# A recommendation tower on one core: top layers in four sets, and one PSUM factor filled by DMA and ScalarE in place of a matmul

## The chip, the cores and the metric

The kernel runs on one core of a Trainium2 chip. The metric is the device time of one execution in microseconds (us). The profile of an execution also has a span, from the first to the last instruction, which is a little shorter than the device time.

## The reference, cut to what matters

512 samples each look up 32 rows of 16 numbers (one row from each of 32 tables). Three layers of products follow, and each layer's output is summed over the 16 columns; the 3 x 64 sums with 16 dense inputs go through three top layers. All is float32.

```python
e = stack([tbl_0[ids[:, 0]], ..., tbl_31[ids[:, 31]]], axis=1)      # 512 x 32 x 16
xk = x0 = e
for W in (W0, W1, W2):                     # 32 x (32 or 64) x 64
    xk = relu(einsum('bmd,bhd,mhk->bkd', x0, xk, W))
    outs.append(sum(xk, axis=2))           # 512 x 64 each
h = concatenate([concatenate(outs, axis=1), dense_ctx], axis=1)     # 512 x 208
h = maximum(h @ W_top1 + b_top1, 0.0)      # 512 x 512
h = maximum(h @ W_top2 + b_top2, 0.0)      # 512 x 256
y = h @ W_top3                             # 512 x 1
```

## The kernel before, in words

The 512 samples are two halves, t = 0 and 1, that are worked side by side in the two halves of TensorE's columns (`side_by_side`, L566). Each half is cut into nine sets p = 0 to 8 of `SAMPLES` = 16, 24, 32 (six times), 24 samples (L16); a set of 32 samples has 512 columns, one of 24 has 384, one of 16 has 256.

A set passes three layers n = 0, 1, 2. Their order is `STAGES` (L41 to L48): (1, p), then (0, p + 1), then (2, p - 1), for each p. So while set p is in layer 1, its successor is in layer 0 and its predecessor in layer 2. "Stage (n, p)" below means layer n of set p.

In each stage a left factor (each of the layer's input rows repeated 4 times over the partitions) is multiplied with rotated copies of the set's gathered rows, and TensorE multiplies the products with the weights and adds them up in `result[n]`. The rotated copies come in two forms (q = 0 and 1, four chunks each): `r0_forms` and `r1_forms`. The left factor has two forms as well, j = 0 (input rows 0 to 31) and j = 1 (rows 32 to 63). VectorE makes units of up to four chunks (`products`, L503, the instruction is L519); GpSimd makes some of the chunks of form j = 1 in pairs (L314 to L328, how many is `pool_chunks`). Layers 1 and 2 have three or four VectorE units (0 and 1 are j = 0, 2 and 3 are j = 1), layer 0 has one. `z_vector` has three buffers (NV), so VectorE can be up to three units ahead of TensorE.

Where the left factor comes from:
- Form 1 lies in PSUM bank `left[:, t, 1]`. For layer 0 ScalarE copies it from `h_form` (`copy_h`, L354), which a DMA loaded with the repetition. For layers 1 and 2 ScalarE issues a DMA that repeats rows 32 to 63 of the previous layer's output in `xj1_forms` (`load_xj1`, L386), and later copies it to PSUM (`copy_xj1`, L364). GpSimd reads `xj1_forms` directly.
- Form 0 of layers 1 and 2 lies in `left[:, t, 0]`. TensorE makes it: `select` (L598) multiplies the previous layer's output with a 0/1 matrix. select(2, p - 1) stands after unit 1 of stage (1, p), select(1, p + 1) after unit 1 of stage (2, p - 1).

ScalarE's order is written out by hand (L443 to L493). For each p: copy_xj1(1, p); copy_h(p + 1); relu(1, p); copy_xj1(2, p - 1); relu(0, p + 1); load_xj1(1, p + 1); relu(2, p - 1); load_xj1(2, p). Each copy waits for its DMA and for the PSUM bank to come free, and what stands behind it waits too.

SyncE's queue (L271 to L290) stores each set's gathered rows to DRAM (`store_x0`), then loads `h_form`, the two `r0_forms` and the two `r1_forms` (1 MB each for 32 samples). The stores wait for the gathers (L309), which GpSimd issues: 20 at once for sets 0 and 1, 16 for set 2 behind a wait for the first select (L335 to L338), and then 8 behind each stage's GpSimd products (L340 to L344). The r loads also wait until layer 2 of the set three before is done.

The top layers are made in two parts, both in tiles cut from a free slot of `r0_forms` (L151 to L163). `early` (L608 on TensorE, L417 on ScalarE) takes sets 0 to 6 (400 columns) in seven steps, spread over stages (2, 7) and (2, 8). The rest, sets 7 and 8 (112 columns, `LATE`), follows when the last layer 2 is done (L668 to L690).

Of the kernel before, what the change touches and what calls it, by code (L numbers as in the profile page):

```python
# [15 lines left out]
SAMPLES = [16, 24] + [32] * 6 + [24]  # L16
NP = len(SAMPLES)
# [9 lines left out]
EARLY = NP - 2  # L27
EARLY_COLUMNS, LATE = 2 * START[EARLY], 2 * (START[NP] - START[EARLY])

# [19 lines left out]
LAYERS = [_stage for _stage in STAGES if _stage[0] > 0]  # L49

# [64 lines left out]
def build(nc, table, ids, base, w0, w0_mirror, not_twice, w12, select, dense, w_top1, b_top1, w_top2, b_top2, w_top3,  # L115
# [3 lines left out]
    with ExitStack() as ctx:  # L119
# [7 lines left out]
        table_base = sb("table_base", [128, GATHERS_BEFORE[-1]], I32)  # L127
# [8 lines left out]
        z_square = sb("z_square", [128, 2, C])  # L136
# [13 lines left out]

        spare = r0_forms[:, (NP - 3) % R0_SLOTS].rearrange("p t s c -> p (t s c)")  # L151
        spare_at = [0]

        def from_spare(columns):
            at = spare_at[0]
            spare_at[0] += columns
            return spare[:, at:at + columns]

        top_in = from_spare(2 * B).rearrange("p (f t c) -> p f t c", f=2, t=2)
        hidden1 = from_spare(N1 * EARLY_COLUMNS).rearrange("p (k c) -> p k c", k=N1)  # L160
        hidden2 = from_spare(N2 * EARLY_COLUMNS).rearrange("p (k c) -> p k c", k=N2)
        late1 = from_spare(N1 * LATE).rearrange("p (k c) -> p k c", k=N1)
        late2 = from_spare(N2 * LATE).rearrange("p (k c) -> p k c", k=N2)  # L163
        y_sb = h_form[0:1, 0].rearrange("o (t b) -> o t b", t=2)
# [4 lines left out]
        y_psum = ctx.enter_context(nc.psum_tensor("y_psum", [128, B], F32))  # L169
        early_banks = [y_psum, result[0]]  # L170
        late1_psum = [left[:, t, 0, 0:2 * LATE].rearrange("p (k c) -> p k c", c=LATE) for t in range(2)]
        late2_psum = [left[:, t, 1] for t in range(2)]
        late3_psum = result[1]
# [14 lines left out]
        selected = sem("selected")  # L188
        left_copied = sem("left_copied")
# [8 lines left out]
        early_in_ready = sem("early_in_ready")  # L198
        early_summed = sem("early_summed")
        early_ready = sem("early_ready")  # L200
# [29 lines left out]
        def _(sp):  # L230
# [61 lines left out]
            for k, samples in enumerate((slice(0, START[EARLY]), slice(START[EARLY], B // 2))):  # L292
                sp.wait_ge(y_ready, k + 1)
                sp.dma_start(out.rearrange("(t b) o -> o t b", t=2)[:, :, samples], y_sb[:, :, samples]
                             ).then_inc(y_stored, 16)
            sp.wait_ge(y_stored, 32)

        @block.gpsimd
        def _(pool):
# [31 lines left out]
            nc.gpsimd.tensor_tensor(row_index[:], ids_all[:], table_base[:], ALU.add).then_inc(index_ready, 1)  # L331
# [15 lines left out]
        def _(act):  # L347
# [24 lines left out]
            def relu(n, p):  # L372
# [4 lines left out]
                if p > 0:  # L377
                    act.wait_ge(x_summed[n], p)
                    if n < 2:

                        act.wait_ge(selected, LAYER_AT[n + 1, p - 1] + 1)
                        for t in range(2):
                            act.wait_ge(xj1_loaded[n][t], 16 * p)
                nc.scalar.activation(x_sb[n][:, 0:columns(p)], result[n][:, 0:columns(p)], ACT.Relu).then_inc(x_ready[n], 1)  # L384

# [14 lines left out]
            def top_block(n, t, pairs, ready):  # L400
                samples = slice(START[pairs[0]], START[pairs[1]])
                nc.scalar.activation(top_in[K * (n % 2):K * (n % 2) + K, n // 2, t, samples],  # L402
                                     d_sums[K * t:K * t + K, n, samples], ACT.Copy).then_inc(ready, 1)

            def y_out(pairs, bank):
                first, end = START[pairs[0]], START[pairs[1]]
                nc.scalar.activation(y_sb[:, :, first:end],
                                     bank[0:1, 0:2 * (end - first)].rearrange("o (t b) -> o t b", t=2),
                                     ACT.Copy).then_inc(y_ready, 1)

            def early_inputs():
                for n in range(3):
                    act.wait_ge(x_summed[n], EARLY)
                    for t in range(2):
                        top_block(n, t, (0, EARLY), early_in_ready)

            def early(k):  # L417
                act.wait_ge(early_summed, k + 1)
                bank = early_banks[k % 2]
                if k < N1:  # L420
                    nc.scalar.activation(hidden1[:, k], bank[:, 0:EARLY_COLUMNS], ACT.Relu,
                                         bias=b_top1_sb[:, k:k + 1]).then_inc(early_ready, 1)
                elif k < N1 + N2:
                    nc.scalar.activation(hidden2[:, k - N1], bank[:, 0:EARLY_COLUMNS], ACT.Relu,
                                         bias=b_top2_sb[:, k - N1:k - N1 + 1]).then_inc(early_ready, 1)
                else:
                    y_out((0, EARLY), bank)

            act.dma_start(table_base[:], base).then_inc(ids_loaded, 16)
# [32 lines left out]

            act.wait_ge(z_vector_ready, 2 * vector_after((2, EARLY - 1)))
            act.wait_ge(z_pool_ready, 2 * pool_after((2, EARLY - 1)))
            act.dma_start(top_in[K:K + D, 1], dense).then_inc(top_loaded, 16)
            early_inputs()
            copy_xj1(2, last - 1)
            relu(1, last)
            load_xj1(2, last)
            act.wait_ge(top_loaded, 16 * 7)  # L470
            for k in range(N1):
                early(k)
            copy_xj1(2, last)
            for n in range(2):
                act.wait_ge(x_summed[n], NP)
                for t in range(2):
                    top_block(n, t, (EARLY, NP), late_in_ready)
            relu(2, last - 1)
            for k in range(N1, N1 + N2 + 1):
                early(k)  # L480
# [3 lines left out]
            top_block(2, 0, (EARLY, NP), late_in_ready)  # L484
            act.wait_ge(late1_summed, 1)
            for k in range(N1 // 2):
                nc.scalar.activation(late1[:, k], late1_psum[0][:, k], ACT.Relu,
                                     bias=b_top1_sb[:, k:k + 1]).then_inc(late1_by_scalar, 1)
            act.wait_ge(late2_summed, 1)
            nc.scalar.activation(late2[:, 0], late2_psum[0][:, 0:LATE], ACT.Relu,  # L490
                                 bias=b_top2_sb[:, 0:1]).then_inc(late2_by_scalar, 1)
            act.wait_ge(late3_summed, 1)
            y_out((EARLY, NP), late3_psum)  # L493

        @block.vector
        def _(dve):
# [6 lines left out]
            def products(n, p, k):  # L503
# [4 lines left out]
                for t in range(2):  # L508
# [6 lines left out]
                    elif k == 0:  # L515
                        dve.wait_ge(selected, LAYER_AT[n, p] + 1)
# [37 lines left out]
            nc.vector.tensor_copy(top_in[0:K, 1, 1, START[EARLY]:START[NP]],  # L554
                                  d_sums[K:2 * K, 2, START[EARLY]:START[NP]]).then_inc(late_in_ready, 1)
            dve.wait_ge(late1_summed, 2)
            for k in range(N1 // 2, N1):
                nc.vector.tensor_scalar(late1[:, k], late1_psum[1][:, k - N1 // 2], b_top1_sb[:, k:k + 1], 0.0,
                                        ALU.add, ALU.max).then_inc(late1_by_vector, 1)
            dve.wait_ge(late2_summed, 2)  # L560
            nc.vector.tensor_scalar(late2[:, 1], late2_psum[1][:, 0:LATE], b_top2_sb[:, 1:2], 0.0,
# [3 lines left out]
        def _(pe):  # L565
# [28 lines left out]
            def squares(p):  # L594
                pe.wait_ge(z_square_ready, 2 * p + 2)
                side_by_side(0, p, w0_sb[:, 4], z_square, False, True).then_inc(z_square_used, 1)
# [11 lines left out]
            def early(k):  # L608
                if k == 0:
                    pe.wait_ge(top_loaded, 16 * 7)  # L610
                    pe.wait_ge(early_in_ready, 6)
                if k == 1:
                    pe.wait_ge(x_ready[0], NP)
                if k >= 2:
                    pe.wait_ge(early_ready, k - 1)
                bank = early_banks[k % 2]
                if k < N1:
                    for half, rows in enumerate((128, K + D)):
                        done = nc.tensor.matmul(  # L619
# [122 lines left out]
```

## Time and profile before

| what | value |
|---|---|
| device time, median of 3 runs | 353.35 us (351.65 to 353.98) |
| device time of the profiled execution | 353.74 us |
| its span | 351.9 us |
| TensorE matmul busy | 305.4 us, 87% |
| VectorE busy | 274.2 us, 78% |
| GpSimd busy | 254.2 us, 72% |
| ScalarE busy | 61.6 us, 18% |
| mean granted TensorE clock | 0.985 of full |

The device time is 1.84 us over the span: what lies around the first and the last instruction. The shares are averages over stages with different limits. A matmul of the program shows as two records in this trace.

### The profile page before, as it was taken

The numbers are of one execution on the slowest core, as the hardware profiler recorded it, in microseconds if no ns is written. First come the engines' busy times: TensorE is split into PE (matmuls) and PEld (weight loads), VectorE is DVE, ScalarE is ACT, GpSimd is POOL, SyncE is SP. The second block draws the span as 40 slices with busy tenths as digits, with TensorE's granted clock in tenths as the row PEclk, the third lists the DMA queues.
The fourth block names the chain that finished last, engine by engine and source line by source line (L and its number), as shares of the span: only waits on it lengthen the run. The fifth ranks groups of instructions, "written<-read, shape, count | busy, mean of one in ns | idle before, by whom it ended". The sixth has DMA issues, their size and how long they took to land. (4 is left out here: it accounts for less than half of the span.)

```text
span 351.9 us, 3914 instructions
## 1 busy us (share of the span) xinstructions
PE 305.4 (87%) x1476; PEld 112.7 (32%) x1476; DVE 274.2 (78%) x173; ACT 61.6 (18%) x122; POOL 254.2 (72%) x193
## 2 busy tenths in 40 slices
PE   0016859798999988999999999999999999998986
PEld 0013513243334222323333333233333334333426
DVE  0024949799999969999999999999999788954201
ACT  1001210301220330012201220222031104113011
POOL 5775678879788988888898879898919567917000
PEclk9999996999999999999999999999999999999998
DMA  5374956957973984286338643952580102100000
GB/s 178 45 251 83 369 111 180 376 88 213 381 149 65 279 329 80 28 337 260 56 71 303 272 72 77 378 190 61 151 327 0 45 2 63 45 2 0 0 0 0
DMA packets 52282, 52.07 MB, mean 148 GB/s; under 512 B 37574, under 2 KB 42568, under 8 KB 49064
## 3 DMA queue, kind: packets, MB, share of 16 engines
q1 hardware_dynamic: 41272, 39.92, 34.2%
q10 hardware_dynamic: 6896, 10.85, 11.5%
q0 software_dynamic: 4096, 1.06, 3.0%
q8 instruction: 11, 0.18, 0.2%
q14 instruction: 7, 0.06, 0.0%
HBM read 41.33 MB, written 2.10 MB: 123 GB/s over the span
## 5 line engine op out<-in xcount | busy, mean ns | idle before, releaser
L519 DVE TENSOR_TENSOR z_vector<-left,r_forms 128x2048 f32<-128x2048 f32 (+3 forms) x140 | 260.0, 1924 | 45.4 <-DMA r_forms<-x_rows 23.0
L569 PE MATMUL result<-z_vector,w_sb 128*64 128x512 f32 (+2 forms) x1056 | 213.9, 557 | 41.5 <-DVE z_vector L519 40.2
L309 POOL DMA_INDIRECT gathered_rows<-table,row_index x128 | 121.8, 951 | 41.2 <-issue 34.5
L324 POOL TENSOR_TENSOR z_pool<-r_forms,xj_forms 128x1024 f32<-128x1024 f32 (+2 forms) x60 | 131.8, 2232 | 24.7 <-PE result L569 15.0
L569 PEld LDWEIGHTS result<-z_vector,w_sb 128*64 128x64 f32 x1056 | 77.3, 142 | 172.9 <-issue 143.4
L569 PE MATMUL result<-z_pool,w_sb 128*64 128x512 f32 (+2 forms) x240 | 51.8, 571 | 0.0
L384 ACT ACTIVATE x_sb<-result 128x512 f32<-128x512 f32 (+2 forms) x27 | 14.9, 551 | 169.7 <-PE result L569 169.7
L499 DVE TENSOR_REDUCE d_sums<-x_sb 128x32 f32<-128x512 f32 (+2 forms) x27 | 16.8, 625 | 20.0 <-ACT x_sb L384 20.0
L569 PEld LDWEIGHTS result<-z_pool,w_sb 128*64 128x64 f32 x240 | 15.7, 136 | 34.1 <-issue 33.2
L368 ACT ACTIVATE left<-xj_forms 128x512 f32<-128x512 f32 (+2 forms) x36 | 18.6, 547 | 17.1 <-DMA xj_forms<-x_sb 6.8
L359 ACT ACTIVATE left<-h_form 128x512 f32<-128x512 f32 (+2 forms) x18 | 10.0, 553 | 59.8 <-DVE z_vector L519 44.9
L604 PE MATMUL left<-x_sb,select_sb 64*128 64x512 f32 (+2 forms) x72 | 19.1, 609 | 1.2 <-ACT x_sb L384 1.2
L604 PEld LDWEIGHTS left<-x_sb,select_sb 64*128 64x128 f32 x72 | 5.7, 191 | 14.5 <-issue 13.3
L362 ACT ACTIVATE z_square<-h_form 128x512 f32<-128x512 f32 (+2 forms) x18 | 10.2, 567 | 0.0
L569 PE MATMUL result<-z_square,w_sb 128*64 128x512 f32 (+2 forms) x36 | 8.9, 573 | 0.0
L569 PEld LDWEIGHTS result<-z_square,w_sb 128*64 128x64 f32 x36 | 2.8, 147 | 4.5 <-issue 4.5
L525 DVE TENSOR_TENSOR w_sb<-w_sb,w_extra 128x192 f32<-128x192 f32 x1 | 0.4, 359 | 4.5 <-DMA fold_mask<-not_twice 4.5
L402 ACT ACTIVATE r_forms<-d_sums 64x200 f32<-64x200 f32 (+1 forms) x11 | 3.4, 313 | 1.1 <-DVE d_sums L499 0.6
L672 PE MATMUL left<-r_forms,w_top_sb 128*128 128x112 f32 (+1 forms) x16 | 2.2, 296 | 1.5 <-ACT r_forms L402 1.5
L683 PEld LDWEIGHTS left<-r_forms,w_top_sb 128*128 128x128 f32 x16 | 3.4, 326 | 0.0
L683 PE MATMUL left<-r_forms,w_top_sb 128*128 128x112 f32 x16 | 3.4, 406 | 0.0
L619 PE MATMUL result<-r_forms,w_top_sb 128*128 128x400 f32 (+1 forms) x8 | 3.2, 525 | 0.0
(32 smaller groups left out, 28.1 us busy)
## 6 DMA issues: line engine op xcount, KB each, us to landing
r_forms<-x_rows SPq DMA_DIRECT2D x24, 1024.0 KB, 10.4
r_forms<-x_rows SPq DMA_DIRECT2D x8, 768.0 KB, 6.8
xj_forms<-x_sb ACTq DMA_DIRECT2D x24, 256.0 KB, 4.0
h_form<-x_rows SPq DMA_DIRECT2D x12, 256.0 KB, 3.0
gathered_rows<-table,row_index POOLq DMA_INDIRECT x128, 3.3
r_forms<-x_rows SPq DMA_DIRECT2D x4, 512.0 KB, 6.1
x_rows<-gathered_rows SPq DMA_DIRECT2D x24, 64.0 KB, 2.5
xj_forms<-x_sb ACTq DMA_DIRECT2D x8, 192.0 KB, 3.1
```

The source lines that it names most:

```text
L309: nc.gpsimd.indirect_dma_start(gathered_rows[:, half % GATHERED, g], None, table, bass.IndirectOffsetOnAxis(ap=row_index[:, at:at + 1], ax ...
L324: nc.gpsimd.tensor_tensor(z_pool[:, unit % NZP, t, :, 0:columns(p)], r_form(q, p, t)[:, s0:s1], xj1_forms[form_buffer(n, p)][:, t, 0:colum ...
L359: nc.scalar.activation(left[:, t, 1, 0:columns(p)], h_rows, ACT.Copy).then_inc(left_copied, 1)
L362: nc.scalar.activation(z_square[:, t, 0:columns(p)], h_rows, ACT.Square).then_inc(z_square_ready, 1)
L368: nc.scalar.activation(left[:, t, 1, 0:columns(p)], xj1_forms[form_buffer(n, p)][:, t, 0:columns(p)], ACT.Copy).then_inc(left_copied, 1)
L384: nc.scalar.activation(x_sb[n][:, 0:columns(p)], result[n][:, 0:columns(p)], ACT.Relu).then_inc(x_ready[n], 1)
L402: nc.scalar.activation(top_in[K * (n % 2):K * (n % 2) + K, n // 2, t, samples], d_sums[K * t:K * t + K, n, samples], ACT.Copy).then_inc(re ...
L499: nc.vector.tensor_reduce(d_sums[:, n, START[p]:START[p + 1]], x_sb[n][:, 0:columns(p)].rearrange("p (b d) -> p b d", d=D), AXIS.X, ALU.ad ...
L519: nc.vector.tensor_tensor(z_vector[:, unit % NV, t, 0:s1 - s0, 0:columns(p)], left[:, t, bank, 0:columns(p)].unsqueeze(1).broadcast_to([12 ...
L569: done = nc.tensor.matmul(result[n][K * t:K * t + K, 0:columns(p)], weights, z[:, t, 0:columns(p)], start=first, stop=last)
L604: done = nc.tensor.matmul(left[:, t, 0, 0:columns(p)], select_sb[K * t:K * t + K], x_sb[n - 1][K * t:K * t + K, 0:columns(p)], start=True, ...
L683: done = nc.tensor.matmul(late2_psum[m][:, 0:LATE], w_top2_sb[:, k, 128 * m:128 * m + 128], late1[:, k], start=k == 0, stop=k == N1 - 1)
```

## The change

- The sets are 16, 16 and seven times 32 samples: set 1 gives 8 of its 24 samples (per half) to set 8.
- Form 0 of the left factor of layer 2 is no longer made by `select`. ScalarE issues a DMA that repeats rows 0 to 31 in a new tile `xj0_form` (`load_xj0`, two DMAs of 256 KB, just ahead of those of `load_xj1(2, p)`), and copies it to `left[:, t, 0]` (`copy_xj0`). The copy stands behind copy_xj1(1, p) and ahead of copy_h(p + 1). Layer 1 keeps its select.
- The top layers are made in four sets of 64 samples per half (128 columns), after sets 2, 4, 6 and 8 are done. The first three are whole: 16, 16 and 4 matmul records. Set one is spread over stages (2, 3), (1, 5), (2, 4); set two over (2, 5), (1, 7), (2, 6); set three over (2, 7) and (2, 8). The first half of the last set's first top layer is made inside stage (2, 8). Each set's output is stored by a DMA from ScalarE's queue.
- They have tiles of their own. To make room, `z_square` is gone (ScalarE squares `h_form` in place, and the next load of `h_form` waits for TensorE's squares), `table_base` is gone, and `dynamic_dma_scratch_size` is 4096 for 8192.

```diff
-SAMPLES = [16, 24] + [32] * 6 + [24]
+SAMPLES = [16, 16] + [32] * 7
...
+GROUP_ENDS = [3, 5, 7, 9]
+TOP1_AT = [4, 6]
+GS = B // 8
+GC = 2 * GS
...
+BY_DMA = [_stage for _stage in LAYERS if _stage[0] == 2]
+SELECTED = [_stage for _stage in LAYERS if _stage not in BY_DMA]
...
-                    sp.wait_ge(z_square_ready, 2 * (p - 1) + t + 1)
+                    sp.wait_ge(z_square_used, p)
...
-                    if p > 0:
-                        act.wait_ge(z_square_used, p)
-                    nc.scalar.activation(z_square[:, t, 0:columns(p)], h_rows, ACT.Square).then_inc(z_square_ready, 1)
+                    act.wait_ge(left_copied, left_copies((0, p), t))
+                    nc.scalar.activation(h_rows, h_rows, ACT.Square).then_inc(z_square_ready, 1)
...
+            def load_xj0(n, p):
+
+                at = BY_DMA.index((n, p))
+                act.wait_ge(x_ready[n - 1], p + 1)
+                if at > 0:
+                    act.wait_ge(left0_copied, 2 * at)
+                for t in range(2):
+                    rows = x_sb[n - 1][K * t:K * t + H, 0:columns(p)]
+                    act.dma_start(xj0_form[:, t, 0:columns(p)], rows.unsqueeze(1).broadcast_to([H, DELTAS, columns(p)])
+                                  ).then_inc(xj0_loaded[t], 16)
+
+            def copy_xj0(n, p):
+                at = LAYER_AT[n, p]
+                for t in range(2):
+                    act.wait_ge(xj0_loaded[t], 16 * (BY_DMA.index((n, p)) + 1))
+                    if at > 0:
+
+                        act.wait_ge(z_vector_ready, 2 * VECTOR_BEFORE[LAYERS[at - 1]] + 3 + t)
+                    nc.scalar.activation(left[:, t, 0, 0:columns(p)], xj0_form[:, t, 0:columns(p)], ACT.Copy
+                                         ).then_inc(left0_copied, 1)
...
             for p in range(NP - 1):
                 copy_xj1(1, p)
+                if p > 0:
+                    copy_xj0(2, p - 1)
                 copy_h(p + 1)
+                if p - 1 in TOP1_AT:
+                    top_hidden2(TOP1_AT.index(p - 1))
                 relu(1, p)
...
+                if p in TOP1_AT:
+                    group = TOP1_AT.index(p)
+                    load_dense(group)
+                    top_inputs(group, range(3))
+                    top_hidden1(group)
+                if p - 1 in TOP1_AT:
+                    group = TOP1_AT.index(p - 1)
+                    act.wait_ge(top3_summed, group + 1)
+                    top_out(group, top3_psum)
                 if p > 0:
                     relu(2, p - 1)
+                load_xj0(2, p)
                 load_xj1(2, p)
...
-                        dve.wait_ge(selected, LAYER_AT[n, p] + 1)
+                        if (n, p) in SELECTED:
+                            dve.wait_ge(selected, SELECTED.index((n, p)) + 1)
+                        else:
+                            dve.wait_ge(left0_copied, 2 * BY_DMA.index((n, p)) + t + 1)
...
+            def top1(group):
+
+                for k in range(N1):
                     for half, rows in enumerate((128, K + D)):
...
+                        done = nc.tensor.matmul(top1_psum[k], w_top1_sb[0:rows, half, 128 * k:128 * k + 128],
+                                                top_in[0:rows, half], start=half == 0, stop=half == 1)
+                done.then_inc(top1_summed, 1)
...
-                layer(1, p, {1: [lambda: select(2, p - 1)]} if p > 0 else {})
+                made, ended = p in TOP1_AT, p - 1 in TOP1_AT
+                layer(1, p, {1: [lambda: top2(TOP1_AT.index(p - 1))]} if ended else {})
                 vector_unit(0, p + 1, 0)
                 squares(p + 1)
+                if ended:
+                    top3(TOP1_AT.index(p - 1))
                 if p > 0:
-                    layer(2, p - 1, {1: [lambda: select(1, p + 1)]})
+                    layer(2, p - 1, {1: [lambda: select(1, p + 1)],
+                                     "pool": [lambda: whole_top1(TOP1_AT.index(p))] if made else []})
...
-            layer(1, last, {1: [lambda: select(2, last - 1)]})
-            early(0)
-            layer(2, last - 1, {0: [lambda: early(1)], 1: [lambda: select(2, last), lambda: early(2)],
-                                "pool": [lambda: early(3)]})
-            layer(2, last, {0: [lambda: early(N1)], 1: [lambda: early(N1 + 1)], "pool": [lambda: early(N1 + N2)]})
...
+            layer(1, last)
+            whole_top1(2)
+            layer(2, last - 1, {1: [lambda: top2(2)]})
+            layer(2, last, {0: [lambda: top3(2)], "pool": [late_top1_begun]})
...
-    nc = bacc.Bacc("TRN2", target_bir_lowering=False, num_devices=1, dynamic_dma_scratch_size=8192)
+    nc = bacc.Bacc("TRN2", target_bir_lowering=False, num_devices=1, dynamic_dma_scratch_size=4096)
```

## Rows read from the trace of the kernel before

**Rows 1.** GpSimd and VectorE in time, the first 130 us.
```profile
31.61 0.95 POOL L309 DMA_INDIRECT gathered_rows<-table,row_index  x1 [3.01 <-PE left L604]
32.86 0.94 POOL L309 DMA_INDIRECT gathered_rows<-table,row_index  x1 [0.30 <-issue]
...
64.09 2.29 DVE L519 TENSOR_TENSOR z_vector<-left,r_forms 128x2048 f32<-128x2048 f32 x1 [2.28 <-DMA r_forms<-x_rows]
...
97.75 3.62 POOL L324 TENSOR_TENSOR z_pool<-r_forms,xj_forms 128x768 f32<-128x768 f32 x2
...
128.41 2.29 DVE L519 TENSOR_TENSOR z_vector<-left,r_forms 128x2048 f32<-128x2048 f32 x1 [0.35 <-DMA r_forms<-x_rows]
```

**Rows 2.** Chain that ended last, in order of time: start, length, what.
```profile
223.31 2.32 DVE z_vector L519
...
225.67 3.65 PE result L569 x16
229.32 1.06 PE left L604 x4
...
301.06 1.54 PE y_psum L619 x4
...
326.52 2.88 PE y_psum L625 x8
```

**Rows 3.** TensorE in time: start, length, what, [idle before, releaser].
```profile
249.55 3.65 PE L569 MATMUL result<-z_pool,w_sb 128*64 128x512 f32 x16
253.03 10.47 PE L569 MATMUL result<-z_vector,w_sb 128*64 128x512 f32 x48
...
295.68 2.80 PE L569 MATMUL result<-z_pool,w_sb 128*64 128x384 f32 x16
298.31 2.75 PE L569 MATMUL result<-z_vector,w_sb 128*64 128x384 f32 x16
...
323.72 2.80 PE L569 MATMUL result<-z_vector,w_sb 128*64 128x384 f32 x16 [1.31 <-ACT x_sb L384]
...
343.38 2.24 PE L672 MATMUL left<-r_forms,w_top_sb 128*128 128x112 f32 x16 [1.46 <-ACT r_forms L402]
```

**Rows 4.** SyncE's queue (SPq), ScalarE and its queue (ACTq) in time.
```profile
150.12 1.24 SPq L262 DMA_DIRECT2D r_forms<-x_rows  x2
...
151.78 0.60 ACT L384 ACTIVATE x_sb<-result 128x512 f32<-128x512 f32 x1 [15.87 <-PE result L569]
151.87 1.33 ACTq L396 DMA_DIRECT2D xj_forms<-x_sb  x2
...
185.36 1.24 SPq L262 DMA_DIRECT2D r_forms<-x_rows  x2
...
187.06 0.60 ACT L384 ACTIVATE x_sb<-result 128x512 f32<-128x512 f32 x1 [14.35 <-PE result L569]
```

**Rows 5.** VectorE in time, stages (1, 4) and (0, 5): start, length, what.
```profile
156.49 8.88 DVE L519 TENSOR_TENSOR z_vector<-left,r_forms 128x2048 f32<-128x2048 f32 x4
```

**Rows 6.** The page's DMA issues: the gathers, median us to landing.
```profile
gathered_rows<-table,row_index POOLq DMA_INDIRECT x128, 3.3
```

**Rows 7.** Tile xj_forms, 145 to 170 us: its two DMAs and their landing.
```profile
L396 ACTq DMA_DIRECT2D xj_forms<-x_sb x2: 551/651/751, 151.9 to 152.4; - x2
...
DMA to landing us min/median/max: 9.2/10.6/12.0
```

**Rows 8.** DMA queues (packets, MB, share), 151 to 155, then 155 to 159 us.
```profile
q1 hardware_dynamic: 298, 1.49, 101.5%
...
q1 hardware_dynamic: 171, 1.27, 81.1%
q10 hardware_dynamic: 112, 0.23, 14.9%
```

**Rows 9.** The last r0 loads, and the landing of the xj_forms issued at 256.8.
```profile
251.10 1.24 SPq L262 DMA_DIRECT2D r_forms<-x_rows  x2
...
DMA to landing us min/median/max: 6.9/6.9/6.9
```

More of the change, by code:

```diff
@@ L135, in build @@
         z_pool = sb("z_pool", [128, NZP, 2, 2, C])
[L136 removed]
+        xj0_form = sb("xj0_form", [128, 2, C])
         w0_sb = sb("w0_sb", [128, 5, K])
@@ L188, in build @@
         selected = sem("selected")
+        xj0_loaded = [sem(f"xj0_loaded_t{t}") for t in range(2)]
+        left0_copied = sem("left0_copied")
         left_copied = sem("left_copied")
@@ L290, in _ @@
                     load_r1(p, t)
[L292 to L296, printed above, removed]
+            sp.wait_ge(y_stored, 16 * len(GROUP_ENDS))
         @block.gpsimd
@@ new lines, in top_inputs, with top_hidden1 @@
+            def top_inputs(group, layers):
+                for n in layers:
+                    act.wait_ge(x_summed[n], GROUP_ENDS[group])
+                    for t in range(2):
+                        top_block(n, t, group, top_in_ready)
+            def top_hidden1(group):
+                act.wait_ge(top1_summed, group + 1)
+                for k in range(N1):
+                    nc.scalar.activation(hidden1[:, k], top1_psum[k], ACT.Relu,
+                                         bias=b_top1_sb[:, k:k + 1]).then_inc(hidden1_ready, 1)
@@ new lines, in top_hidden2, with top_out @@
+            def top_hidden2(group):
+                act.wait_ge(top2_summed, group + 1)
+                for m in range(N2):
+                    nc.scalar.activation(hidden2[:, m], top2_psum[m], ACT.Relu,
+                                         bias=b_top2_sb[:, m:m + 1]).then_inc(hidden2_ready, 1)
+            def top_out(group, y):
+                if group > 0:
+                    act.wait_ge(y_stored, 16 * group)
+                nc.scalar.activation(y_sb[:], y, ACT.Copy).then_inc(y_ready, 1)
+                act.wait_ge(y_ready, group + 1)
+                act.dma_start(out.rearrange("(t b) o -> o t b", t=2)[:, :, samples(group)],
+                              y_sb[:].rearrange("o (t b) -> o t b", t=2)).then_inc(y_stored, 16)
@@ new lines, in top1, with late_top1 @@
+            def top1(group):
+                for k in range(N1):
+                    for half, rows in enumerate((128, K + D)):
+                        done = nc.tensor.matmul(top1_psum[k], w_top1_sb[0:rows, half, 128 * k:128 * k + 128],
+                                                top_in[0:rows, half], start=half == 0, stop=half == 1)
+                done.then_inc(top1_summed, 1)
+            def late_top1(half):
+                rows = (128, K + D)[half]
+                for k in range(N1):
+                    done = nc.tensor.matmul(late1_psum[k], w_top1_sb[0:rows, half, 128 * k:128 * k + 128],
+                                            top_in[0:rows, half], start=half == 0 and k % 2 == 0,
+                                            stop=half == 1 and k % 2 == 1)
+                    if half == 1 and k % 2 == 1:
+                        done.then_inc(late1_summed, 1)
@@ new lines, in whole_top1, with top2 @@
+            def whole_top1(group):
+                pe.wait_ge(top_loaded, 16 * 6)
+                pe.wait_ge(dense_loaded, 16 * (group + 1))
+                pe.wait_ge(top_in_ready, 6 * (group + 1))
+                if group > 0:
+                    pe.wait_ge(y_ready, group)
+                top1(group)
+            def top2(group):
+                pe.wait_ge(hidden1_ready, N1 * (group + 1))
+                for m in range(N2):
+                    for k in range(N1):
+                        done = nc.tensor.matmul(top2_psum[m], w_top2_sb[:, k, 128 * m:128 * m + 128], hidden1[:, k],
+                                                start=k == 0, stop=k == N1 - 1)
+                done.then_inc(top2_summed, 1)
@@ new lines, in top3, with late_top1_begun @@
+            def top3(group):
+                pe.wait_ge(hidden2_ready, N2 * (group + 1))
+                for m in range(N2):
+                    done = nc.tensor.matmul(top3_psum, w_top3_sb[:, m:m + 1], hidden2[:, m],
+                                            start=m == 0, stop=m == N2 - 1)
+                done.then_inc(top3_summed, 1)
+            def late_top1_begun():
+                pe.wait_ge(top_in_ready, 6 * (len(GROUP_ENDS) - 1) + 4)
+                pe.wait_ge(y_ready, len(GROUP_ENDS) - 1)
+                pe.wait_ge(x_ready[0], NP)
+                late_top1(0)
```

171 lines of the change are left out of this document (61 added, 110 removed).

## The prediction

> **What bounds the kernel now.** I read the page first, then the chain of waits in order of time, then each engine's timeline by stage, and last the DMA landings by tile. The page calls TensorE 87% busy and VectorE 78%, averages that hide three stretches. Up to 128.4 us the gathers and loads set the pace: VectorE waits for a select at the first stages and for r_forms at 64.09 and again just before 128.41 [rows 1]. From there to 225.6 the chain is VectorE's; after 225.67 it is TensorE's without a gap, but for 1.31 us at 323.72 and the tail behind 341.94 [rows 2, 3].
>
> I count from relu(2, p - 1), in ScalarE's order the mark at which the DMAs for stage (2, p) go out. It starts at 151.78 and 187.06 [rows 4]: a phase is 35.3 us, and TensorE's share of it is 148 records and two selects, 34.3 by the pitches below. In the middle both engines are nearly full. VectorE's stage (0, 5) starts two instructions (4.44 us) into the group at 156.49, at 160.93 [rows 5]: 9.15 us after the mark.
>
> **The change, part by part, without its new wait.** Pitches first: 16 records of 512 columns go in 253.03 - 249.55 = 3.48 us, of 384 in 298.31 - 295.68 = 2.63 [rows 3]: 0.054 us more for each record. A top record of 400 columns takes 1.54/4 = 0.385 [rows 2], one of 112 takes 2.24/16 = 0.140 [rows 3]; on the line between them 128 columns take 0.154. So a set of the new top layers is 16 + 16 records (2.5 + 2.5 us) and four for y (0.4): 5.4 us.
> - Selects gone behind 225.67: three of 1.06 us [rows 2] and one of 384 columns, 0.84: -4.0. Those before save nothing where VectorE bounds.
> - The seven early steps go: 4 x 1.54 + 2 x 2.88 [rows 2] and, at the same 0.36 a record, 1.44 for y = 13.4. Top sets two and three come: +10.8. Set one falls where TensorE has slack, 0.8 of the 1.0 above and the 1.06 of a dropped select; 3.5 of its 5.4 us are left as lateness at 225.67: +3.5.
> - Set 8 with 512 columns: 20 + 64 + 64 records x 0.054 = 8.0, its select 0.2: +8.2, on the path, as TensorE bounds there.
> - Set 1 with 256 columns: cheaper by some 3.4 us in (1, 1) and again in (2, 1), but (0, 2) waits for r_forms until 64.09 anyway. Those come from set 2's gathers, and these wait for the first select, at 31.61 [rows 1], which is set 0's and does not move; the four gathers fewer ahead of it only lengthen that 3.01 us wait. What does get earlier is GpSimd: its pairs in (1, 1) and (2, 1) shrink from 3.6 us [rows 1] to some 2.5 by their columns, and the gathers behind them start 1.1 to 2.2 us earlier, which moves 128.41: I take -1.6.
> - Tail: half of the last top1 (8 records, +1.2) moves ahead of the end and out of the tail (-1.0 there), wider columns +0.3; the wait at 323.72 shrinks from 1.31 to a bare relu, -0.5. Together 0.
> - Squares in place, own tiles, fewer waits on early buffers: nothing. load_h then waits for TensorE's squares, which stand a whole stage ahead of it in each phase. ScalarE is 18% busy and carries the additional copies; six top blocks (1.5 us) and the hidden relus stand where it waited for relu(2, p - 1) anyway.
> - The gathers' descriptor scratch is halved. They are 1.25 us apart [rows 1] and land in 3.3 [rows 6], so about three are in flight. Bounds: 0, or, if only two could be in flight, 3.3/2 = 1.65, 0.4 us x 16 a set = 6.4 us for each set while gathers bound. 
>
> **The new wait.** copy_xj0(2, p - 1) makes ScalarE wait for both DMAs of xj0_form, and copy_h(p + 1) stands behind it, for which VectorE waits at (0, p + 1). load_xj0 takes the very place at which load_xj1 is now. There the two DMAs issued at 151.9 and 152.4 needed 9.2 and 12.0 us [rows 7], because SyncE's four 1 MB r loads go out from 150.12 on [rows 4]. From 151 to 155 us the queue of ScalarE moved nothing, from 155 to 159 only 0.23 MB beside 1.27 MB [rows 8]. Nobody minded: xj1 is not needed for 12 us. xj0's second half would be there at 164.4. Then come two copies at 0.6: copy_xj0 ends at 165.0, copy_h at 165.6, 13.8 us behind the mark. VectorE wanted it at 160.93 [rows 5]. So VectorE is stalled 4.7 us.
>
> It doesn't heal by itself, since TensorE's work up to the next mark follows from (0, p + 1). From VectorE's start of (0, 5): 4.44 + 0.6 (a sum) + 8.9 (two units) = 13.9 until (2, 3)'s unit 1 is made; TensorE then 3.5, select 1.06, GpSimd's part 1.8, units 3.5 + 1.7: mark at +25.5, and 2.5 more where top1 stands in it. At +25.5 + 13.8 a phase would be 39.3 for 35.3. But the loads also age: set 6's r loads are released by gathers (185.36 [rows 4], late by some 2.5 as xj1 now lands behind xj0 and holds up GpSimd), the mark is 7 late, so they are 5.8 old instead of 1.7. The row at that age is [rows 9]: r loads out from 251.10, xj at 256.8 lands in 6.9, with 3 MB; a fourth at the 373 GB/s of [rows 8] (1.49 MB in 4 us) adds 2.7. That gives 0.6 + 9.6 + 1.2 = 11.4 behind the mark; the floor is 7.7 (two more DMA issues of 0.6 and one unit of VectorE's). I take 11.4 for p = 5, and 12.5 for p = 6, where the loads wait for VectorE's end of (2, 4), about 4 ahead of the mark.
>
> In times of before: (0, 5) at 165.6; mark 165.6 + 25.5 + 2.5 = 193.6; (0, 6) at 205.0; mark 230.5; (0, 7) at 243.0; mark, with the larger GpSimd part and top1 of set two, + 28.0 = 271.0. From there TensorE is full: two units 7.0, top2 2.5, GpSimd's part 3.5, a unit 3.5: (0, 8) starts at 287.5. Before, it started at 253.03 + 10.4 (48 records) + 1.06 + 3.5 + 3.5 = 271.5: +16.0. Behind it: set 8 +8.2, selects -1.9, early steps -13.4, set three +5.4, y of set two +0.4, tail 0: rounded -1.2. With -1.6 from the start the sum is +13.2; on the profiled execution's 353.74 (span 351.9 and 1.84 around it) that is 366.9, and on the median, 0.39 lower, 366.5.
>
> The Trainium skill, the same page, section "Queues, rings and completion order", says each DMA engine takes turns between queues by packet. In [rows 8] a packet is 5.0 to 7.4 KB on SyncE's queue and 2 KB on ScalarE's, which agrees for the second window; turn about from the issue on would have moved some 0.2 MB in the first as well, where the row has none.
>
> **Rivals.**
> - One stall only: after the first, the loads are so old that xj0 lands inside the floor. For it: the age grows from 1.7 to 5.8. Against: even at 5.7 [rows 9] has 6.9 us with 3 MB. The 4.7 is then in part hidden by the 3.5 of set one's lateness; it gives 356.9 + about 4 = 361.
> - No stall: the sum of the parts, 353.35 + 3.5 = 356.9. It would need xj0 to land in under 8 us with 4 MB ahead. [rows 7] speak against it.
> - Not slower: set 2's gathers are not held by the first select but come 5 us earlier with the four gathers that set 1 loses, r_forms land at 59 and all moves. Without a stall 356.9 + 1.6 - 7.2 = 351.3. It decides if GpSimd's first gather of set 2 starts before 30 us. The 3.01 us wait at 31.61 [rows 1] speaks against.
>
> **How the numbers follow.** Forecast (stall in each of three or four phases) 0.60, one stall 0.17, no stall 0.13, not slower 0.10. A change of 1% (3.5 us) is about what a measurement of this kernel can tell. Not slower gives faster 0.05 and same 0.05; no stall lies on the border, 0.06 same and 0.07 slower. Faster 0.05, same 0.11, slower 0.84. The range: up to 373 with 13.8 behind every mark (+2.6, +1.3) and the stall growing with set one's top layers; down to 355, which leaves out most of the last case.
>
> **What would show it.** Right: copy_h(5) to (7) released by the xj0 DMA, late; VectorE idle 3 to 5 us ahead of three (0, p) stages, put down to copies by ScalarE; landing of xj0_form over 8 us there and 3 to 4 elsewhere; (0, 2) still at about 64. Wrong: VectorE's groups without gaps from 130 to 225 us; r_forms of set 2 before 62; gathers further apart than 1.25 us. The number would also fall if r loads were released so late that xj0 goes ahead of them, as at 114.

## The result and the profile after

The change makes the kernel slower: 370.25 us (median of 4, 369.00 to 372.13) against 352.58 us (median of 4, 351.65 to 353.98), 1.050 times the time of before (95% interval 1.044 to 1.056). The forecast was 366.5 us, in a range of 355 to 373; it started from the three runs of the kernel before that had been measured by then (median 353.35). The profiled execution took 370.41 us, its span is 368.6.

From the page of the profile: the engines and the granted clock of TensorE.

```profile
span 368.6 us, 4081 instructions
PE 300.8 (82%) x1512; PEld 116.3 (32%) x1512; DVE 273.7 (74%) x173; ACT 76.3 (21%) x166; POOL 256.1 (69%) x193
PEclk9998998599999989999999999999999899999998
```

TensorE has less to do than before (305.4 us were busy) and VectorE as much (274.2), and the span is 16.7 us longer: the time is in waits, and in matmuls at the lower clock. Where they are is seen in ScalarE's timeline, beside [rows 4], and in VectorE's.

ScalarE and its queue from relu(2, 2) on:

```profile
154.05 0.60 ACT L384 ACTIVATE x_sb<-result 128x512 f32<-128x512 f32 x1 [14.34 <-PE result L615]
154.12 1.21 ACTq L394 DMA_DIRECT2D xj_form<-x_sb  x2
...
162.60 0.60 ACT L404 ACTIVATE left<-xj_form 128x512 f32<-128x512 f32 x1 [4.69 <-DMA xj_form<-x_sb]
166.48 0.60 ACT L404 ACTIVATE left<-xj_form 128x512 f32<-128x512 f32 x1 [3.28 <-DMA xj_form<-x_sb]
167.01 0.58 ACT L357 ACTIVATE left<-h_form 128x512 f32<-128x512 f32 x1
```

VectorE, the starts of stages (0, 5) to (0, 8):

```profile
167.69 4.49 DVE L566 TENSOR_TENSOR z_vector<-left,r_forms 128x2048 f32<-128x2048 f32 x2 [4.68 <-issue]
...
205.57 4.49 DVE L566 TENSOR_TENSOR z_vector<-left,r_forms 128x2048 f32<-128x2048 f32 x2 [2.14 <-issue]
...
242.84 4.49 DVE L566 TENSOR_TENSOR z_vector<-left,r_forms 128x2048 f32<-128x2048 f32 x2 [2.36 <-issue]
...
284.21 4.49 DVE L566 TENSOR_TENSOR z_vector<-left,r_forms 128x2048 f32<-128x2048 f32 x2 [5.55 <-issue]
```

L384 is a relu (the one at 154.05 is relu(2, 2), the prediction's mark), L404 is copy_xj0, L357 copy_h. ScalarE stands 4.69 and 3.28 us for the two xj0 DMAs, then makes copy_h at once; VectorE starts 0.1 us after copy_h ends, having stood 4.68 us. Its gap is labelled "issue", since the profile shows no event that ended it; the releaser has to be read from ScalarE's rows. This is the wait that the prediction named; it comes four times, the last time ahead of (0, 8), where the prediction counted on none.

A second loss lies ahead of that. GpSimd, VectorE and TensorE in the first 135 us, as in [rows 1]:

```profile
31.47 0.94 POOL L307 DMA_INDIRECT gathered_rows<-table,row_index  x1 [7.88 <-PE left L651]
...
63.19 2.29 DVE L566 TENSOR_TENSOR z_vector<-left,r_forms 128x2048 f32<-128x2048 f32 x1 [7.84 <-DMA r_forms<-x_rows]
...
68.87 6.58 PE L615 MATMUL result<-z_vector,w_sb 128*64 128x512 f32 x16 [10.30 <-DVE z_vector L566]
...
132.92 5.29 PE L615 MATMUL result<-z_vector,w_sb 128*64 128x512 f32 x16 [4.27 <-DVE z_vector L566]
```

As forecast, the gathers of set 2 still start at 31.5, behind a wait now of 7.88 us, and VectorE's (0, 2) at 63. But TensorE has then been idle for 10.30 us, and its 16 records take 6.58 us where 16 at the full clock take 3.65; those of (0, 4) at 132.92 take 5.29. Such a group is called a slow unit below. The stretches show the clock (columns: stretch and its length, busy us of PE, PEld, DVE, ACT, POOL with counts, granted clock, DMA share, GB/s):

```profile
60.00:66.00 6.00, 0.00 (x0) 0.00 (x0) 2.29 (x1) 1.30 (x4) 5.04 (x6) 0.60 1.01 400
66.00:72.00 6.00, 3.13 (x8) 0.99 (x10) 5.47 (x4) 0.39 (x1) 4.93 (x6) 0.50 0.88 275
```

0.50 is 1.2 GHz, the lower of the two levels. In the next stretch, 72 to 78 us, TensorE works without a pause and the mean is 0.77. The Trainium skill ("TensorE: Matmul & The Clock Gate", Part 1) calls the throttled state the default, from which activity releases the engine; the trace agrees in these three stretches. Ahead of the first matmul the clock column doesn't show it, as it has 1.00 there; the durations do: the first 16 records, of 256 columns at 25.39, take 3.68 us, and 16 such at 43.02 take 1.95.

### The profile page after: what moved, and what is told of

Read it like the earlier page. It is cut to its first block, busy times and chain, and to the rows that moved or that the text cites. A ratio compares the mean times of both kernels' runs of the same rounds, so it can differ in the third digit from the quotient of the medians.

```text
span 368.6 us, 4081 instructions
## 1 busy us (share of the span) xinstructions
PE 300.8 (82%) x1512; PEld 116.3 (32%) x1512; DVE 273.7 (74%) x173; ACT 76.3 (21%) x166; POOL 256.1 (69%) x193
## 3 DMA queue, kind: packets, MB, share of 16 engines
q10 hardware_dynamic: 9664, 15.05, 14.9%
q0 software_dynamic: 4096, 1.06, 2.7%
## 4 chain that ended last, share of the span: by engine, by line
PE 54%; DMA 18%; DVE 12%; issue 8%; POOL 5%; SPq 1%; ACT 1%; ACTq 0%; DVEq 0%; POOLq 0%
PE result L615 47%; DVE z_vector L566 12%; DMA r_forms<-x_rows 6%; DMA xj_form<-x_sb 5%; POOL gathered_rows L307 5%; DMA x_rows<-gathered_rows 4%; DMA gathered_rows<-table,row_index 3%; PE left L651 2%; PE top_psum L659 2%; PE top_psum L685 1%; PE left L748 1%; DMA row_index<-base 1%; DVE d_sums L543 1%; ACTq L394 0%; ACT x_sb L384 0%
## 5 line engine op out<-in xcount | busy, mean ns | idle before, releaser
L566 DVE TENSOR_TENSOR z_vector<-left,r_forms 128x2048 f32<-128x2048 f32 (+2 forms) x140 | 259.1, 1909 | 68.3 <-DMA r_forms<-x_rows 31.8
L615 PE MATMUL result<-z_vector,w_sb 128*64 128x512 f32 (+1 forms) x1056 | 217.4, 562 | 60.9 <-DVE z_vector L566 60.1
L322 POOL TENSOR_TENSOR z_pool<-r_forms,xj_forms 128x1024 f32<-128x1024 f32 (+1 forms) x60 | 133.9, 2268 | 41.9 <-DMA xj_forms<-x_sb 28.7
L307 POOL DMA_INDIRECT gathered_rows<-table,row_index x128 | 121.5, 949 | 45.9 <-issue 34.8
L615 PE MATMUL result<-z_pool,w_sb 128*64 128x512 f32 (+1 forms) x240 | 52.4, 575 | 1.6 <-POOL z_pool L322 1.6
L384 ACT ACTIVATE x_sb<-result 128x512 f32<-128x512 f32 (+1 forms) x27 | 14.8, 549 | 135.4 <-PE result L615 135.3
L365 ACT ACTIVATE left<-xj_forms 128x512 f32<-128x512 f32 (+1 forms) x36 | 19.1, 549 | 46.7 <-DVE z_vector L566 26.6
L543 DVE TENSOR_REDUCE d_sums<-x_sb 128x32 f32<-128x512 f32 (+1 forms) x27 | 16.5, 617 | 15.0 <-ACT x_sb L384 15.0
L404 ACT ACTIVATE left<-xj_form 128x512 f32<-128x512 f32 (+1 forms) x18 | 9.6, 549 | 32.2 <-DMA xj_form<-x_sb 31.7
L357 ACT ACTIVATE left<-h_form 128x512 f32<-128x512 f32 (+1 forms) x18 | 9.8, 544 | 30.2 <-DMA h_form<-x_rows 26.2
L359 ACT ACTIVATE h_form<-h_form 128x512 f32<-128x512 f32 (+1 forms) x18 | 10.5, 583 | 0.6
```

Source lines behind the costliest of these rows:

```text
L307: nc.gpsimd.indirect_dma_start(gathered_rows[:, half % GATHERED, g], None, table, bass.IndirectOffsetOnAxis(ap=row_index[:, at:at + 1], ax ...
L322: nc.gpsimd.tensor_tensor(z_pool[:, unit % NZP, t, :, 0:columns(p)], r_form(q, p, t)[:, s0:s1], xj1_forms[form_buffer(n, p)][:, t, 0:colum ...
L359: nc.scalar.activation(h_rows, h_rows, ACT.Square).then_inc(z_square_ready, 1)
L365: nc.scalar.activation(left[:, t, 1, 0:columns(p)], xj1_forms[form_buffer(n, p)][:, t, 0:columns(p)], ACT.Copy).then_inc(left_copied, 1)
L543: nc.vector.tensor_reduce(d_sums[:, n, START[p]:START[p + 1]], x_sb[n][:, 0:columns(p)].rearrange("p (b d) -> p b d", d=D), AXIS.X, ALU.ad ...
L566: nc.vector.tensor_tensor(z_vector[:, unit % NV, t, 0:s1 - s0, 0:columns(p)], left[:, t, bank, 0:columns(p)].unsqueeze(1).broadcast_to([12 ...
```

## The experiments

The theories: A, the wait for the xj0 DMA in ScalarE's order ahead of copy_h. B, the set sizes. C, the additional 4 MB of DMA traffic, whoever waits for it. The runs were measured on three chips, e1 to e4 on the first, e5, e6, e7 and e9 on the second, the others on the third, each beside the kernel of before. On the second chip that kernel itself took 362.78 us (29 runs) instead of 352.4, so what was measured there is compared by its ratio alone. A ratio is always to the kernel of before on the same chip, with its 95% interval.

**e1: select back.**

```diff
-BY_DMA = [_stage for _stage in LAYERS if _stage[0] == 2]
+BY_DMA = []
...
+                layer(1, p, {1: ([lambda: select(2, p - 1)] if p > 0 and (2, p - 1) in SELECTED else [])
+                             + ([lambda: top2(TOP1_AT.index(p - 1))] if ended else [])})
```

(and likewise for the last two sets; load_xj0 and copy_xj0 return at once)

> The changed kernel with layer 2's form 0 made by TensorE's select again (no xj0_form DMA, no copy of it); sizes 16, 16, 32 x 7 and the four top sets stay. Theory A (the wait for the xj0_form DMA, in ScalarE's order ahead of copy_h, is the main cost): VectorE's gaps of 4.7, 2.1, 2.4 and 5.5 us ahead of (0, 5) to (0, 8) are gone, some 10 us less for 4 to 5 us of selects back: 360 to 363 us. Theory B (the sizes are the cost: a late fall of the clock at 69 us and more work at the end): hardly any gain, 368 or more. Theory C (additional DMA traffic, whoever waits for it): like A here.

Measured: 361.74 us (4 runs) beside 352.44 of before, ratio 1.024 (1.018 to 1.031). The four gaps are gone: 8.5 us, as A (and C) said. What is left over before, 9.3 us, belongs to the sizes and the top sets (e7 will show that the top sets alone cost nothing). The slow unit at 68.55 (6.16 us, after 10.41 idle) is there as well, so it isn't the DMA's doing.

**e2: the copy behind copy_h.** The whole edit:

```diff
                 copy_xj1(1, p)
+                copy_h(p + 1)
                 if p > 0:
                     copy_xj0(2, p - 1)
-                copy_h(p + 1)
```

> The changed kernel with one line moved: copy_xj0(2, p - 1) behind copy_h(p + 1) on ScalarE in the loop, so that VectorE's (0, p + 1) does not wait for the xj0_form DMA. All traffic and all copies stay. Theory A: 357 to 361 us, the four gaps ahead of (0, 5) to (0, 8) under 1 us each. Theory C (traffic): the gaps turn up as waits for r_forms, h_form or xj1_forms elsewhere, 366 or more. Theory B: 368 or more.

Measured: 359.97, 360.04, 364.96 and 366.40 us. Without the last the ratio is 1.025 (1.015 to 1.035) for 1.050 of the changed kernel, so some 9 us come from one line; with four runs so far apart that is good to 4 us, and A's 357 to 361 is neither met nor missed clearly. The gaps ahead of (0, 5) to (0, 7) are gone. But the profiled execution was the one of 366.40, so the rest is only indicated there: 5.01 us for a copy of xj1 at 268.68 and 5.38 for r_forms at 278.55, set 8's, whose gathers come late. That part would be C's, at the one place where set 8 has grown; it is not shown further.

**e3: sizes of before.**

```diff
-SAMPLES = [16, 16] + [32] * 7
+SAMPLES = [16, 24] + [32] * 6 + [24]
```

> The changed kernel with the set sizes of before (16, 24, 32 x 6, 24); DMA, copy and four top sets stay. Theory A with the sizes as second cost: the gaps ahead of (0, 5) to (0, 7) stay; what goes is set 8's 8 us on TensorE and the 3 to 4 us that the first 130 us lost to a slower granted clock at 69 us: 357 to 361 us. Theory B: all comes back, 353 or less. If the sizes cost nothing: 370.

Measured: 358.96 us, ratio 1.019 (1.011 to 1.027): 11 us from the sizes. The gaps stay (5.07, 3.19 and 2.42 us), as A said. The slow unit did not go: 6.55 us at 69.40, after 3.35 idle. So the 3 to 4 us of the start were not what came back here: e3's mark relu(2, 2) is at 153.87, the changed kernel's at 154.05. What came back is set 8's work and its DMA wait: from the fourth mark, relu(2, 5), to the end e3 takes 84.6 us and the changed kernel 97.9.

**e4: the DMA half alone.** The kernel of before with load_xj0, copy_xj0 ahead of copy_h, and squares in place:

```diff
+BY_DMA = [_stage for _stage in LAYERS if _stage[0] == 2]
...
                 copy_xj1(1, p)
+                if p > 0 and (2, p - 1) in BY_DMA:
+                    copy_xj0(2, p - 1)
                 copy_h(p + 1)
...
             for k in range(N1):
                 early(k)
+            copy_xj0(2, last)
             copy_xj1(2, last)
```

> The kernel of before with only the second half of the change: xj0_form by DMA, copied by ScalarE ahead of copy_h, squares in place. Sizes, top layers and scratch as before. Theory A: gaps ahead of (0, 5) to (0, 7), 358 to 362 us. Theory B: faster than before by the selects, 349 to 352. Theory C: as A, but with the gaps put down to r_forms.

Measured: 368.01 us, ratio 1.044 (1.035 to 1.052): 15.6 us, more than A expected. The gaps are 5.40, 4.10 and 2.59 us, with units at the low clock behind the first two (5.00 us at 173.90 and 5.35 at 212.90, against 3.65). A had left out the clock: e4 has a slow unit at (0, 2) too (6.12 us at 69.25), and its marks are 3.0, 8.0, 12.2 and 14.9 us behind those of before. And a second wait of the same kind had been built in: copy_xj0(2, 8) stood behind the four early relus. VectorE's timeline there:

```profile
335.21 6.75 DVE L557 TENSOR_TENSOR z_vector<-left,r_forms 128x1536 f32<-128x1536 f32 x4 [11.16 <-ACT left L411]
```

11.16 us of VectorE, of which 2.66 reached TensorE.

**e6: the same with both copies moved,** behind copy_h and behind the first early relu (shown against e4).

```diff
                 copy_xj1(1, p)
+                copy_h(p + 1)
                 if p > 0 and (2, p - 1) in BY_DMA:
                     copy_xj0(2, p - 1)
-                copy_h(p + 1)
...
-            for k in range(N1):
+            early(0)
+            copy_xj0(2, last)
+            for k in range(1, N1):
                 early(k)
-            copy_xj0(2, last)
```

> The kernel of before with the xj0_form DMA, copied behind copy_h (and for the last set behind the first early relu instead of the last): sizes and top layers as before. Theory A: the 15 us that the DMA cost ahead of copy_h are gone, and the selects' 3 to 4 us behind 225 us are won: 349 to 353 us. Theory C: 357 or more.

Measured: ratio 0.999 (0.996 to 1.002; 10 runs, second chip). From 1.044 to 0.999, with all the traffic still there, though on another chip. The selects' 3 to 4 us were not won in the total. From its fourth mark on the profile does show 92.5 us for 95.2 before, 2.7 less; 0.9 of it is lost between the first mark and the fourth.

**e7: the four top sets alone** (e1 with the sizes of before).

> The kernel of before with only the four top sets (and their tiles, squares in place, half the scratch): select makes layer 2's form 0, sizes as before. By the steps of the prediction with the measured 4.5 us for a set: -13.4 + 9.0 + some 4 of lateness from set one - 1 at the tail = -1.5: 350 to 353 us. If set one's top layers were free in VectorE's stretch: 347. If the halved scratch or the squares in place cost something: above 354, with gathers more than 1.25 us apart.

Measured: ratio 0.999 (0.997 to 1.002; 12 runs, second chip). No gain in time: the -1.5 us expected would be 0.996, just below the interval. The profile shows both halves: its three phases from the first mark to the fourth (36.8, 36.8 and 36.3 us) take 5.1 us more than those of before, and the rest 7.0 less (88.2 for 95.2). The gathers are 1.25 us apart (33.75, 34.99, 36.24), so half the descriptor scratch does not delay their issue. (The 16-byte descriptors of the prediction's estimate stand in the Trainium skill, "DMA: Bandwidth & Descriptors", under "Terms", not in the section that it names.)

e1 and e7 differ in the sizes alone: 1.024 and 0.999, so without the DMA the sizes cost 8.8 us.

**e9: the form-0 DMA for the last two sets alone,** on e7.

```diff
-BY_DMA = []
+BY_DMA = [_stage for _stage in LAYERS if _stage[0] == 2 and _stage[1] >= NP - 2]
```

> e7 with the form-0 DMA for stages (2, 7) and (2, 8) alone, where SyncE loads nothing and the landing was 3 to 4 us. Theory A: the DMA is harmless there and TensorE wins two selects, 1.06 + 0.84: 1.5 to 2 us below e7. Theory C (any use of the DMA costs): at or above e7.

Measured: ratio 0.994 (0.992 to 0.996; 12 runs), 360.74 beside e7's 361.98: 1.2 us, a little under the expected 1.5 to 2, and the two intervals do not overlap. Where SyncE loads nothing, the DMA in place of the select pays.

**e5 and e12: sizes of before and the copy behind copy_h,** both edits of e2 and e3, on two chips.

> The changed kernel with the set sizes of before and copy_xj0 behind copy_h: traffic, copies and four top sets stay. Theory A (the order of the wait on ScalarE, plus the sizes): the gaps of 5.1, 3.2 and 2.4 us ahead of (0, 5) to (0, 7) go, and with them the slow unit behind the first; 350 to 354 us. Theory C (the 4 MB of additional traffic delays r_forms, x0_rows and xj1_forms, whoever waits): 356 or more, with gaps put down to those loads.

> e5 once more, now beside the changed kernel: sizes of before, all of layer 2 by DMA, copied behind copy_h. Theory A: 0.99 of the kernel of before, and 3 to 6% below e10.

Measured: ratio 0.990 (0.985 to 0.995; second chip) and 0.9925 (0.989 to 0.996; 349.37 us, 12 runs, beside 352.35), and 5.6% under the changed kernel on the same chip (e10). This version beats both kernels, the one of before by less than 1%, clear of the noise on both chips. Its ScalarE timeline at the place shown above:

```profile
151.72 0.60 ACT L384 ACTIVATE x_sb<-result 128x512 f32<-128x512 f32 x1 [15.87 <-PE result L615]
...
158.81 0.60 ACT L357 ACTIVATE left<-h_form 128x512 f32<-128x512 f32 x1 [3.14 <-DVE z_vector L566]
...
164.79 0.60 ACT L404 ACTIVATE left<-xj_form 128x512 f32<-128x512 f32 x1 [2.03 <-DMA xj_form<-x_sb]
```

and VectorE's:

```profile
156.44 8.87 DVE L566 TENSOR_TENSOR z_vector<-left,r_forms 128x2048 f32<-128x2048 f32 x4
```

The DMA is no faster (its view by tile):

```profile
L394 ACTq DMA_DIRECT2D xj_form<-x_sb x2: 551/590/629, 151.8 to 152.4; - x2
...
DMA to landing us min/median/max: 12.4/12.4/12.4
```

The copy of the second half starts 13.1 us behind the mark (164.79), in the changed kernel 12.4 (166.48); but copy_h starts at 158.81, and VectorE runs its four instructions without a gap, as in [rows 5]. The mark at 151.72 is that of before (151.78), the next is 188.66. With e3 beside it (same code but for the order) the same marks are 153.87 and 196.78: 2.15 us late at the first, from its slow unit at the start, and 8.12 at the second, so in one phase the order is worth 6.0 us; 2.5 of it are e3's slow unit behind the gap (6.12 us at 172.68). At the end the medians are 9.6 apart (358.96 to 349.37, on two chips whose kernels of before agree within 0.1 us); in how many of e3's executions the slow unit stood, and so how much of the 9.6 is its, isn't known beyond the profiled one.

**e10: the changed kernel again,** the yardstick on the third chip.

> The changed kernel itself, as a yardstick beside the others of this call: 1.05 times the kernel of before if the chip is like the first one; where the kernel of before itself loses its first 60 us to the clock or the loads, the ratio is smaller, since part of what the change loses there is lost by both.

Measured: 370.16 us, ratio 1.0505 (1.0445 to 1.0564); before 352.35 (23 runs).

**e8: four gathers more** ahead of the wait for the first select, in the changed kernel:

```diff
-            gather(0, GATHERS_BEFORE[4])
+            gather(0, GATHERS_BEFORE[4] + 4)
...
-                gather(GATHERS_BEFORE[4] + 4 * k, GATHERS_BEFORE[4] + 4 * k + 4)
+                if k < 3:
+                    gather(GATHERS_BEFORE[4] + 4 * k + 4, GATHERS_BEFORE[4] + 4 * k + 8)
```

> The changed kernel with 20 gathers instead of 16 ahead of GpSimd's wait for the first select, as before the change. If the start is lost because set 1's smaller share leaves TensorE idle ahead of (0, 2) and its granted clock then falls, (0, 2) starts some 5 us earlier, the idle time ahead of it halves, and the slow unit there (6.6 for 3.65 us) goes: 5 to 8 us below e10. If the start is set by SyncE's loads instead: within 2 us of e10.

Measured: 363.55 us, 6.6 us under e10. TensorE's rows, of this kernel and then of e10:

```profile
64.99 6.52 PE L616 MATMUL result<-z_vector,w_sb 128*64 128x512 f32 x16 [6.90 <-DVE z_vector L567]
```

```profile
70.36 6.32 PE L615 MATMUL result<-z_vector,w_sb 128*64 128x512 f32 x16 [10.82 <-DVE z_vector L566]
```

The start is 5.4 us earlier, which is most of the gain, but the slow unit did not go: the half of the expectation on the clock was wrong. The idle time ahead of it shrank only to 6.90 us. The gathers' chain is what a change of the first sets must respect.

**e11: the form-0 DMA for sets 6 to 8 alone,** else as e12.

```diff
-BY_DMA = []
+BY_DMA = [_stage for _stage in LAYERS if _stage[0] == 2 and _stage[1] >= NP - 3]
```

> Sizes of before, four top sets, copy_xj0 behind copy_h, and the form-0 DMA for stages (2, 6) to (2, 8) alone; the others by select. If the DMA pays only behind 225 us, where TensorE sets the pace: at or below e12, 0.985 to 0.992 of the kernel of before. If dropping the select pays in the middle as well: 1 to 3 us above e12.

Measured: 349.87 us, ratio 0.9935 (0.990 to 0.997), the same as e12 within the intervals. So where VectorE sets the pace the DMA in place of the select neither costs nor pays, once nobody waits for it.

## Why the prediction was right, and where it was off

The direction, the size and the mechanism held. By its own steps, from mark to mark (a mark is the relu(2, p - 1) at which the DMAs for stage (2, p) go out), in the span's times (forecast with the -1.6 us of the start; measured from ScalarE's relus and VectorE's and TensorE's starts):

| step | forecast | measured |
|---|---|---|
| mark relu(2, 2) at | 150.2 | 154.05 |
| to VectorE's (0, 5) | 13.8 | 13.64 |
| to the next mark, with top1 | 28.0 | 27.83 |
| to (0, 6) | 11.4 | 10.05 |
| to the mark | 25.5 | 25.73 |
| to (0, 7) | 12.5 | 11.54 |
| to the mark, with top1 | 28.0 | 27.83 |
| to TensorE's (0, 8) | 16.5 | 18.08 |
| to the end of the span | 79.2 | 79.85 |
| sum | 365.1 | 368.6 |

The last step comes so close partly by luck: its set three took 0.9 us less than forecast, and the slow unit that opens it 1.7 more. (The terms behind (0, 8) add up to -1.3, not to the -1.2 of the prediction.)

- **The stall.** Right to 0.2 us at the first phase, since both landings stood in [rows 7]. The later ones were taken 1.0 to 1.4 us too long (ageing works a little better than estimated). The sign "VectorE idle 3 to 5 us ahead of three stages" was met only at the first: 4.68, then 2.14, 2.36 and 5.55 us. e12 shows the cause: a landing as late, other order, no stall. "One stall only" and "no stall" fall, "not slower" too: the gathers of set 2 started at 31.47, not before 30.
- **The term mis-sized: the start.** "I take -1.6" was +2.3. The prediction had no term for the clock and none for what the xj0 DMAs do to the loads. GpSimd did get 1.1 us shorter pairs, but (0, 2) ran at half clock behind 10.30 us of idle TensorE, 2.9 us more for its unit. (That the idle time was the cause is not shown: see the last section.) That made the select and the xj1 DMA of stage (1, 2) later, and GpSimd stood 3.80 us for it at 80.93, where before it began at 78.48. A second piece is C's: e1, with the slow unit but without these DMAs, has its mark at 152.12, which splits the 3.9 us about evenly (one profile of each). In the changed kernel the last store of set 4's rows took 6.10 us against a page median of 2.5, as it went out at 114.46, just behind the four xj DMAs of 112.85 to 117.23. These 3.9 us are the whole distance from 365.1 to 368.6 and 0.4 more.
- **The last set.** TensorE was not full ahead of (0, 8), as "from there TensorE is full" said: VectorE's fourth stall of 5.55 us left it idle for 2.26, and the unit behind that took 5.35 us.
- **A set of the top layers** took 1.98 + 1.98 + 0.53 = 4.5 us, not 5.4: the line through 400 and 112 columns gave 0.154 a record, and it is 0.124. The point at 112 columns came from the last stretch, where the page of the profile has the clock at 8 tenths. Set one's lateness was taken at 3.5; in e12, which like the changed kernel has no select there, and where copy_h waits for no DMA, its two phases are 36.9 and 35.8 us long for 35.3 and 34.8 before, 2.6 in all. In e1, with the selects, it is 4.1.
- **The sizes** were forecast at +8.2 for set 8 and -1.6 for the start. Where select makes the factor they cost 8.8 us by the ratios of e1 and e7, and from the fourth mark on 96.9 us for 88.2: there the 8.2 was nearly right. With the DMA they cost 11.0 (changed kernel and e3) and 11.5 (e2 and e12, by the ratios). Most of the surplus lies at (0, 8): VectorE's fourth stall, and behind it 2.26 us of idle TensorE and 1.7 of slow unit, are not in e3. Why the stall is not in e3 was not isolated.

Open: the second chip. All four kernels profiled there (e5, e6, e7, e9) have the relu of (0, 1) at 57.0 to 57.5 us; before has it at 47.72, e12 at 47.73. e5 and e12 are the same kernel on two chips, 9.6 us apart by their medians. ScalarE in e5:

```profile
57.21 0.49 ACT L384 ACTIVATE x_sb<-result 128x384 f32<-128x384 f32 x1 [4.71 <-remote]
```

In e12 it is released by TensorE; so nearly the whole difference is there by then. In e5 TensorE's records of (0, 1) end at 49.86, with the granted clock at 1.00 from 24 to 54 us, and the relu starts 7.3 us later: it isn't the clock but a release that comes later, by an event that the profile can't name ("another core or an unknown queue"). No profile of the kernel of before was taken there, so it isn't known whether that cost hides a gain of e6 and e7.

## What to carry to other kernels

A DMA in place of a matmul is judged by its landing at that very place in the order, not by the median of its size: here the same 256 KB take 3.9 us, or 12 where 4 MB from another queue are in flight. In an in-order engine the copy that waits for it belongs behind every copy that is needed sooner; this one line was worth some 9 us in both pairs, by their ratios (the changed kernel to e2, e3 to e12). And making an early set smaller doesn't start the next one earlier when that one's gathers wait for something else; it only makes the idle time longer. All five profiles of that kind (the changed kernel, e1, e2, e8, e10; 6.9 to 11.7 us idle) have a slow unit behind it.

## What the runs showed of the hardware

- Idle time ahead does not by itself decide the clock. The unit of (0, 2) took 6.55 us after 3.35 idle in e3 and 3.65 us after 3.65 idle in e12. TensorE's work up to there is the same in both; they differ in ScalarE's order (the line of e2) and in the chip. The same unit was slow after 3.96 idle in e4, and at full clock after 2.25 before and 2.24 in e11. TensorE in e3, then in e12:

```profile
69.40 6.55 PE L615 MATMUL result<-z_vector,w_sb 128*64 128x512 f32 x16 [3.35 <-DVE z_vector L566]
```

```profile
69.15 3.65 PE L615 MATMUL result<-z_vector,w_sb 128*64 128x512 f32 x16 [3.65 <-DVE z_vector L566]
```

- The same kernel of before took 352.4 us on two chips and 362.8 on another (29 runs, 359.9 to 364.1). A difference of 1% must come from runs on the same chip.
- A DMA of ScalarE's queue issued just behind the start of SyncE's 4 MB landed 12.4 us later even in the fastest kernel; moving the copy changed who waits, not the landing.
